# Softmax denominators with part of their sum on GpSimd, and the second norm's work in another place

## The reference

```
x = x + gated(group_norm(x))                 # a gate from mean, max, std of each channel and their median
t = tokens(x)                                # (8, 256, 512)
n = layer_norm(t)
q, k, v = n @ wq.T, n @ wk.T, n @ wv.T       # 16 heads of 32
s = 30 * tanh(q k^T / (sqrt(32) * 30))       # mask: key <= query and query - key < 256
t = t + softmax(s) v @ wo.T
n = layer_norm(t)                            # the "second norm"
t = t + top2_of_8_experts(n) + shared_expert(n)
```

## Time and profile before

| | |
|---|---|
| median of 3 runs | 732.54 us (731.76 to 732.93) |
| the profiled execution, its own time | 731.98 us |
| span of its profile | 730.2 us |
| busy: PE, DVE, POOL, ACT | 649.6, 390.4, 285.0, 280.4 us |
| granted TensorE clock, mean over the span | 0.96 |

### The profile page before, as it was taken

How to read it: one execution, slowest core, us unless ns; L and a number is a source line. 1 busy time by engine, 2 the same in 40 slices (tenths; PEclk the granted TensorE clock), 3 DMA queues, 4 the chain that set the end, 5 groups by cost and what they waited for, 6 DMA issues and landing times.

```text
span 730.2 us, 13493 instructions
## 1 busy us (share of the span) xinstructions
PE 649.6 (89%) x4866; PEld 525.6 (72%) x4867; DVE 390.4 (53%) x895; ACT 280.4 (38%) x498; POOL 285.0 (39%) x329
## 2 busy tenths in 40 slices
PE   0213989999999999999999999999899999999992
PEld 0203978888888888887789899998576767676671
DVE  7775454657575757572646994224444444434441
ACT  7641263636363636364533123434112121121210
POOL 1340153333333333332321115857245455454534
PEclk9955999999999999999999999999999999999997
DMA  9800000101010101020216333442755555655443
GB/s 309 325 0 0 1 2 1 59 2 57 0 57 0 57 0 57 0 88 1 80 68 244 115 99 112 142 156 68 268 111 95 106 101 100 107 96 109 93 70 43
DMA packets 24641, 62.07 MB, mean 85 GB/s; under 512 B 3040, under 2 KB 7904, under 8 KB 23072
## 3 DMA queue, kind: packets, MB, share of 16 engines
q1 hardware_dynamic: 14768, 41.16, 15.8%
q0 software_dynamic: 9168, 20.45, 15.2%
q10 hardware_dynamic: 672, 0.03, 0.1%
HBM read 38.56 MB, written 23.07 MB: 84 GB/s over the span
## 4 chain that ended last, share of the span: by engine, by line
PE 83%; DVE 8%; DMA 3%; issue 2%; POOL 1%; ACT 1%; SPq 1%; DVEq 0%; POOLq 0%; ACTq 0%
PE scores L1488 26%; PE PS L1488 25%; PE scores L1841 9%; PE PS L1597 6%; PE scores L1760 5%; PE scores L1583 3%; PE PS L1784 2%; PE PS L1548 2%; DMA wd_sb<-in_wd 2%; DMA T<-in_x 1%; PE PS L1832 1%; PE PS L1537 1%; DVE front L984 1%; DVE qT L910 1%; POOL w_l L510 1%
## 5 line engine op out<-in xcount | busy, mean ns | idle before, releaser
L1488 PE MATMUL scores<-xb,sw_h 128*128 128x256 f32 x512 | 94.5, 285 | 0.1
L629 POOL DMA_INDIRECT out_tokens<-yo,dest x36 | 57.1, 1586 | 84.2 <-DMA out_tokens<-yo,dest 80.7
L1488 PEld LDWEIGHTS scores<-xb,sw_h 128*128 128x128 f32 x512 | 81.2, 192 | 2.5 <-issue 0.8
L1488 PE MATMUL PS<-xt_h,w_h 128*128 128x256 f32 x256 | 75.4, 295 | 1.5 <-DVE xt_l L1126 1.5
L864 ACT ACTIVATE es<-scores 128x256 f32<-128x256 f32 x39 | 14.9, 383 | 160.9 <-PE scores L1488 160.9
L1841 PE MATMUL scores<-wd_sb,ehT 128*128 x156 | 73.6, 594 | 2.1 <-DMA wd_sb<-in_wd 1.1
L534 POOL TENSOR_SCALAR_AFFINE_SELECT probs<-probs 128x256 f32<-128x256 f32 x128 | 51.9, 431 | 56.9 <-ACT probs L731 56.0
L1488 PE MATMUL PS<-xt_l,w_h 128*128 128x256 f32 x256 | 73.2, 286 | 0.0
L1488 PE MATMUL PS<-xt_h,w_l 128*128 128x256 f32 x256 | 73.1, 285 | 0.0
L1488 PE MATMUL scores<-xb,sw_l 128*128 128x256 f32 x256 | 72.5, 283 | 0.0
L1141 DVE RECIPROCAL rden<-PS 128x256 f32<-128x256 f32 x32 | 56.2, 1755 | 24.2 <-PE PS L1597 24.2
(11 more groups left out here) (286 smaller groups left out, 1443.5 us busy)
## 6 DMA issues: line engine op xcount, KB each, us to landing
wgu_l<-in_wgu SPq DMA_DIRECT2D x8, 1024.0 KB, 6.7
T<-in_x SPq DMA_DIRECT2D x8, 512.0 KB, 7.8
w_in<-in_wqkvo SPq DMA_DIRECT2D x4, 1024.0 KB, 12.5
x_rows<-x SPq DMA_DIRECT2D x8, 512.0 KB, 2.8
x_cols<-x2T SPq DMA_DIRECT2D x8, 512.0 KB, 2.7
xc<-x_cols SPq DMA_DIRECT2D x8, 512.0 KB, 3.4
out_tokens<-T SPq DMA_DIRECT2D x8, 512.0 KB, 7.5
wd_sb<-in_wd SPq DMA_DIRECT2D x8, 512.0 KB, 7.1
```

What stands on the lines that cost most here:

```text
L629: pool.indirect_dma_start(out[:, :], bass.IndirectOffsetOnAxis(dest[:, t:t + 1], 0), yo[:, t % 3, :], None, compute_op=ALU.add).then_inc(y ...
L1488: ins = pe.matmul(out, lhs(k, a), rhs(k, b), start=m == 0, stop=m == len(products) - 1)
```

## The change

1. Each `mask` on GpSimd also waits for its own selects (new semaphore `masked_late`) and adds the two key blocks of queries 128 to 255 into a new tile `late_sum` (4 x 2 x 128); `mask_done` is counted up after that add.
2. `head_values`: the products with v stay. Those with ones are 128 columns each: one with the early queries' block of keys 0 to 127, one with `late_sum`.
3. The order: GpSimd's `rstd_of` for the second norm comes behind mask 3 instead of between masks 1 and 2 (in `last_step` it stays); DVE's `second_out` comes behind the copy of Q0; on PE gate_transposes come behind K0, gate_partial behind the scores of pairs 6 and 7, gate_logits behind values 2. The ring's list follows.
4. `late_sum` lies over tiles that only the first 65 us use, and the area in front of the attention's tiles grows by 24 elements.

```diff
-STEP = ["OP0", "OP1", "XN0", "XN1", "Q0", "X2T0", "X2T1", "K0", "GT", "Q1", "K1", "V0", "V1", "YT0", "YT1"]
+STEP = ["OP0", "OP1", "XN0", "XN1", "Q0", "K0", "X2T0", "X2T1", "GT", "Q1", "K1", "V0", "V1", "YT0", "YT1"]
...
-        PROBS, SMALL, BATCH = 4 * 2 * 384, 1840, CB * S
+        PROBS, SMALL, BATCH = 4 * 2 * 384, 1864, CB * S
...
+        scope = area("late_sums", PROBS)
+        late_sum = sb("late_sum", [P, 4, 2, P], fp32, scope)
+        scope.close()
...
-                ins.then_inc(mask_done, 1)
+                ins.then_inc(masked_late, 1)
+                pool.wait_ge(masked_late, 8 * b + p + 1)
+                t = probs[:, p % 4, :].rearrange("p (h q) -> p h q", h=2)
+                pool.tensor_tensor(late_sum[:, p % 4, :, :], t[:, :, P:S], t[:, :, S:S + P],
+                                   ALU.add).then_inc(mask_done, 1)
...
             def step(b, has_next):
-                mask(b, 0)
-                mask(b, 1)
+                for p in range(4):
+                    mask(b, p)
                 if not (isinstance(b, int) and b == 0):
                     rstd_of(var2_ready, rstd2_ready, b - 1)
-                mask(b, 2)
-                mask(b, 3)
                 att_low(b, 0)
...
                 normalise(b, 0, first)
+                if has_front:
+                    project_out(part, "Q0", b)
                 if has_back:
                     second_out(b - 1)
-                if has_front:
-                    project_out(part, "Q0", b)
...
-                for off, lhs in ((0, lambda h, tt: v[:, tt, h * D:(h + 1) * D]), (S, lambda h, tt: ones[:, 0:D])):
-                    for tt in range(TT):
-                        for j in range(HC):
-                            h = HC * c + j
-                            pr = probs[:, (h // 2) % 4, 384 * (h % 2):384 * (h % 2 + 1)]
-                            ins = pe.matmul(od_bank[j * D:(j + 1) * D, off + tt * P:off + S], lhs(h, tt),
-                                            pr[:, 0:S] if tt == 0 else pr[:, S:S + P], start=tt == 0, stop=tt == TT - 1,
-                                            skip_group_check=True)
+                for tt in range(TT):
+                    for j in range(HC):
+                        h = HC * c + j
+                        pr = probs[:, (h // 2) % 4, 384 * (h % 2):384 * (h % 2 + 1)]
+                        pe.matmul(od_bank[j * D:(j + 1) * D, tt * P:S], v[:, tt, h * D:(h + 1) * D],
+                                  pr[:, 0:S] if tt == 0 else pr[:, S:S + P], start=tt == 0, stop=tt == TT - 1,
+                                  skip_group_check=True)
+                for tt in range(TT):
+                    for j in range(HC):
+                        h = HC * c + j
+                        early = probs[:, (h // 2) % 4, 384 * (h % 2):384 * (h % 2) + P]
+                        ins = pe.matmul(od_bank[j * D:(j + 1) * D, S + tt * P:S + (tt + 1) * P], ones[:, 0:D],
+                                        late_sum[:, (h // 2) % 4, h % 2, :] if tt else early, start=True, stop=True,
+                                        skip_group_check=True)
...
                 head_values(b, 1, first)
-                if has_back:
-                    gate_transposes(part, b - 1, b)
                 if has_front:
                     heads_projection(part, "K0", b)
                 if has_back:
-                    gate_partial(part, b)
+                    gate_transposes(part, b - 1, b)
                 head_scores(b, 6, first)
                 head_scores(b, 7, first)
                 if has_back:
+                    gate_partial(part, b)
+                head_values(b, 2, first)
+                if has_back:
                     gate_logits(part, b - 1, b)
-                head_values(b, 2, first)
```

More of the change, by code:

```diff
@@ L169, in layer_kernel @@
         probs = sb("probs", [P, 4, 2 * 384], fp32, scope)
+        row = sb("row", [1, 8, B * UP], fp32, scope)
+        g_avg = sb("g_avg", [P, P], fp32, scope)
+        spread = sb("spread", [P, B * UP], fp32, scope)
+        col = sb("col", [B * UP, 24], fp32, scope)
+        sb("below_rden", [P, 8], fp32, scope)
         rden = sb("rden", [P, S], fp32, scope)
@@ L330, in layer_kernel @@
             sem("scores_full"), sem("tanh_done"), sem("exp_done"), sem("mask_done"))
+        masked_late = sem("masked_late")
         pv_done, att_ready, att_h_done, att_l_done = (
```

## The result

The changed kernel takes 734.62 us in the median of 16 runs (732.41 to 735.57), the kernel before 732.15 (731.20 to 733.15) in 16 runs on the same chips. The ratio is 1.0027 (95% interval 1.0018 to 1.0037): slower by 0.27%. The forecast was 731.2, and no change or a gain were both given more than a loss. The profiled execution took 734.92 us, with a span of 733.2 us for 730.2 before.

What follows compares the result with a forecast made beforehand. PE (TensorE) was taken to bound the kernel, with 83% of the chain. Terms -5 x 0.60 - 1.14 + 0.75 + 2.0 = -1.4 us on the 732.54 median gave 731.2 us, range 728.3 to 734.0.

Steps and rivals of the forecast that it cites:

- The middle steps: Batches 1 to 6: a step of batches 1 to 5 gains 0.60 us, batch 6, having no affine, 1.14.
- What goes from PE: Ones products in head_values: narrowing the wide ones saves 0.217 us a call, 0.87 us a batch.
- What the new order saves on PE: PE's order in a step: fewer changes between product forms save 0.27 us, bounds 0.1 and 0.35.
- Values 3: Middle steps: PE waits 0.54 us for DVE's att, 0.44 of it from the affine colliding with GpSimd's add; bounds 0 and 0.8.
- the rival without a collision: Middle steps, values 3: pair 7's add doesn't hold the affine, wait only 0.1 us; total 728.7 us, chance 0.20.
- Values 1: Middle steps: mask and add end just as PE arrives, no slack left, wait 0 (0 to 0.1) us.
- Dear adds: Rival at values 1, batch 0 and batch 7: mask and add cost 1.08 us for 0.81; total 736.5, chance 0.12.
- Batch 0: First batch: adds lengthen PE's wait for masks by 1.62 us, narrow products return 0.87, net +0.75 us.
- clock: Rival in batch 0: the longer pause, 3.5 us, halves TensorE's clock, losing 1.70 us; total 732.9, chance 0.25.
- Batch 7: Last batch: later masks and adds delay values 2, values 2 and 3 return 0.43; +2.0 us (1.2 to 3.0).
- I leave it as it is: Batch 7, behind PE's wait for mask 5: the existing half-clock loss, read as 1.70 us, is kept unchanged.
- Values 2: Batch 7: begins 2.4 us later, from 0.58 delay, 1.62 for two adds and some 0.2 for collision on DVE.

Runs made afterwards that it cites:

- experiment 7: Changed kernel with the new order only, without adds and with the wide ones products: 730.57 us against 731.79 for the kernel before, ratio 0.9985.
- experiment 4: Changed kernel with DVE's affine moved from behind gate_top to behind the copy of K0: 730.76 us against 731.70 for the kernel before, ratio 0.9988.
- experiment 5: Changed kernel with 24 unused products filling PE's pause in batch 0: 731.47 us against 731.79 for the kernel before, ratio 0.9997.
- experiment 6: Changed kernel with 20 unused products ahead of values 2 in batch 7: 730.49 us against 731.79 for the kernel before, ratio 0.9984.
- 1: Changed kernel with adds and narrow ones products only in batches 1 to 6: 726.54 us against 731.70 for the kernel before, ratio 0.9937.
- Experiment 10: Changed kernel with DVE's split_low moved earlier in batch 7, adds everywhere: 732.48 us against 732.64 for the kernel before, ratio 1.0006.
- experiment 8: Changed kernel's adds and narrow products, but the old order on all three engines: 737.56 us against 731.79 for the kernel before, ratio 1.0087.
- the best kernel: Changed kernel with adds and narrow products only in batches 1 to 6, affine behind K0's copy: 724.66 us against 732.64 for the kernel before, ratio 0.9899.

## Why the prediction was wrong

One reading is a slip on which nothing hangs: beside PE, show two busy engines at 54 to 63% (ACT and DVE), not three.

**The middle steps: right.** -4.17 us for -4.14: five steps of -0.63 (forecast -0.60) and batch 6 with -1.00 (forecast -1.14), by two errors that nearly cancel. *What goes from PE*, 0.217 us a call, stands. *What the new order saves on PE* was taken at 0.27 and is 0.15 (experiment 7), inside its bounds of 0.1 and 0.35. *Values 3* was given a wait of 0.54 and has 0.34 (0.55 us from the product ahead of it, 0.21 before). Of it, the collision is as told:

```profile
184.44 0.77 POOL L540 TENSOR_SCALAR_AFFINE_SELECT probs<-probs 128x256 f32<-128x256 f32 x2
185.30 0.73 POOL L545 TENSOR_TENSOR late_sum<-probs 128x256 f32<-128x256 f32 x1
```

```profile
185.25 1.90 DVE L1096 TENSOR_SCALAR front<-T,coefA,coefB 128x256 f32 x4 [0.30 <-DVE topi L1177]
187.07 1.75 DVE L1149 RECIPROCAL rden<-PS 128x256 f32<-128x256 f32 x1
```

Pair 7's add runs from 185.30 to 186.03 inside the affine, which takes 1.90 us for 1.48, 0.42 where the forecast had 0.44; the rival without a collision is out, and experiment 4 took the wait away with 0.31 us a step. The other 0.1 of the wait wasn't there: on PE's side there are 6.39 us from the logits to values 3, not 6.28, as the opening of Q1 had been taken off twice. Values 1 wait 0.06 us more, where 0 (to 0.1) was said. *Dear adds* are out as well; line 545 over the whole profile, count and min/median/max:

```profile
L545 POOL TENSOR_TENSOR late_sum<-probs x64: 722/734/1572, 95.2 to 360.1; 128x256 f32<-128x256 f32 x64
```

**Batch 0: the step that failed is "clock".** The wait is right, 3.53 us for 3.5, and so is its sum of +0.75 (0.68 with the clock held, experiment 5). The forecast kept the clock at 1.00, on one profile in which it had stayed there through a pause of 1.92 us, and gave its fall 0.25. It fell, for 6.8 us, and cost 2.7 us, where the rival reckoned 1.7 from the 3.4 us stretch of batch 7. So the rival's 732.9 was 1.0 us too low in this term as well.

**Batch 7: +3.83 for +2.0, and the step that failed is the clause "I leave it as it is", of the clock.** With the clock held (experiment 6 against 1) the adds cost 1.93 us, the forecast's work term. That too is a cancellation. Values 0 wait 0.81 us more, as forecast. Values 2 begin 3.3 us later in the step, not 2.4: the collision on DVE was put at 0.2, from no row, and is 0.84 for pair 5's add behind `split_low` and 0.37 for mask 5 (1.14 us for 0.77) beside `second_out`. 0.58 + 1.62 + 0.84 + 0.37 = 3.41, 0.13 more than measured. In the middle step the forecast had reckoned what GpSimd does to DVE; here DVE holds GpSimd. Experiment 10 shows that for the add. No run takes `second_out` away from the mask, but in experiment 8 it was again a mask beside `second_out` that took 1.14 us. The Trainium skill (GPSIMD Engine Reference, Key points) names as contending with GpSimd both DVE's instructions of a 2-port mode and those with two SBUF inputs; the trace agrees, with 0.42 us onto DVE's affine and 0.84 onto GpSimd's add. The forecast weighed the first kind only.

Against this loss stands a gain that the forecast didn't know: the wait of 1.02 us (1.22 less 0.20) behind values 2 is gone once these come later. So 3.38 - 0.44 (narrow products of values 2 and 3) - 1.02 = 1.92, with 3.38 from experiment 6 against 1. The clock makes the difference. Before, it cost 0.67 us, as the slow PE used up that wait. Now it costs 2.57: the half clock lasts twice as long, and the wait is gone already. That is +1.90, where the forecast had 0; with the 1.6 to 1.9 us of the four other profiles it would be +0.9 to +1.2.

**The sum, corrected**: -4.17 + 0.68 + 2.73 + 1.93 + 1.90 = +3.07. The median moved by +2.47, and the two profiled executions by +2.94. It stands 4.5 us over the forecast of -1.4, and the two clock terms are 4.6; with a clock that cost what it did before, the change would be at some -1.6. That the clock is not the same in each execution is seen in the changed kernel's runs, five at 732.4 to 733.3 us and eleven at 734.1 to 735.6. All of the eleven have a mean clock of 0.985 (one 0.957), all of the five 0.987 (one 0.959). The 0.002 between them are what one stretch of 3.4 us makes, half of 3.4 in 733. Whether it is missing in batch 0 or in batch 7 is not known, since none of the five has a profile.

**The chances.** 0.18 for slower was too little. The two clock terms were treated as one rival at one place, though batch 7 had shown in the very rows used what a pause does there, and its pause was to grow by more than that of batch 0.

## What to carry to other kernels

A pause of PE that grows can cost more than its length (in batch 0, 1.6 us of pause and 2.7 of clock): look up where a pause stands, how long it gets, and what PE must do right after it, and price a stretch at half clock there by whether waits behind it absorb it. A change that pays in a loop's middle steps may not pay in the first and the last, where another engine sets the pace; try it without them (here +0.27% becomes -0.63%). Before adding work to GpSimd, list what DVE issues in those microseconds, and move aside first what collides (here `affine`, which with the adds kept to the middle steps made -1.0%, and `split_low`). And do not judge a change by one profile where the clock falls in some executions only: compare the mean granted clocks of the runs as well.

## What the runs showed of the hardware

- Granted clock: with PE idle for 3.5 to 3.6 us in batch 0 it went to half in each profile, for 6.8 us or (once) 3.4. After the pause of 1.9 us it did so in three of five, for 3.4 us. One profile says little of whether it falls in the next execution.
- 24 products of no use, 3.1 us long, kept the clock at 1.00 and were worth 2.2 us net; 20 in batch 7 were worth 3.1 in the median and 2.6 in the profile. Two fills at once were worth 4.3, and the fill in the best kernel nothing.
- The same 3.4 us at half cost 1.5 us in batch 0 (38.01 for 36.48) and 0.67 in batch 7, where a wait behind it took up the rest. Where none did, half clock cost 0.44 to 0.47 us for each microsecond of it behind the end of the pause, in both batches and in all profiles with an empty pause in front; the part within the pause cost nothing.
- An add of 128x256 on GpSimd took 1.57 us for 0.73 beside one DVE instruction with two inputs of 128x1024 (1.42 us), and ended 0.57 us after it. With that instruction moved away it took 0.73.
